# Masked cross-attention: the last key's term taken per group on the extracted output instead of per batch by a product with the identity

## The chip, the cores and the metric

The kernel runs on one core of a Trainium2 chip. The metric is the device time of one execution in microseconds; the time given is the median of three runs. Nothing else runs on the core.

## The reference

A stack of six layers works on `x`, 128 batches of 32 tokens with 256 features (4096 tokens); only the first layer is changed here. It is an attention of the tokens on a context of 257 rows per batch, with 16 heads of 16 features:

```python
q = split_heads(layernorm(x) @ Wq + bq)        # 16 heads x 32 queries x 16
k = split_heads(ctx @ Wk + bk)                 # 16 heads x 257 keys x 16
v = split_heads(ctx @ Wv + bv)
scores = einsum('bhqd,bhkd->bhqk', q, k) / sqrt(16)
scores = where(mask > 0, -1e9, scores)
p = softmax(scores, axis=-1)
x = x + (einsum('bhqk,bhkd->bhqd', p, v) merged to 256) @ Wo + bo
```

After it come a state space layer, a quantized feed-forward layer, a second (sigmoid) attention on the same context, a self-attention and a layer of experts. Everything is float32 within a small tolerance.

## The kernel before

Each layer is one block of code in which every engine has its own instruction stream, written out by hand, and waits on semaphores that the others raise. Nothing is scheduled by a planner: the order on an engine is the order in the code. The changed layer is `masked_attention` (tiles print as `x_...`).

Of the 257 keys, 256 fill two tiles of 128, and the last (`LAST`) stands apart. Its key vectors (`kx`) and value vectors (`vx`) are computed once for all 128 batches in `last_keys`, before the loop. Its score comes from tiny products in `last_scores`, and `place_last` copies it as a 257th column into `prob`, so that the softmax covers it.

The batches go in groups of four, since 4 x 32 tokens fill 128 rows. The loop `for b in SLOTS` has one turn per batch, on every engine. A turn (a slot) on TensorE is: `scores(b)`, `keys(b + 2)`, `turn(b - 1)` (the transposes of the probabilities), `values(b)`, `attend(b - 2)`. By the batch's number in its group one piece of group work is put in: slot 0 has `output` (after the scores) and `xnT`, slot 1 `queries`, slot 2 `denominators`, slot 3 `last_scores`. Slots 0 and 2 have the extraction of two batches' outputs on ScalarE and VectorE (`extract`).

How the last key's value term gets into the output: GpSimd (`value_last`) multiplies the batch's row of `vx`, spread to all 128 partitions by a transfer (`load_vx`), by the probabilities of the last key; partition 32h + t of `prob` holds head h of a strip and query t. `attend` (L492 on) first does eight products of V with the transposed probabilities, adding up in PSUM (`psO`), and then four products of that `pv` tile with the identity, which transpose and add it. Each product is 64 output rows by 128 columns, in float32. `extract` then picks each head's own columns out of `psO` into `oT`. The softmax denominators come at the end: `shares` takes reciprocals of the row sums (`sm`), `spread_sums` on GpSimd spreads them with `eye_q` into `sums`, `denominators` multiplies `sums` by `head_rows` so that each share reaches the rows of its head in `psA`, and `normalise` on VectorE multiplies `oT` by `psA`. `hi_ob` and `lo_ob` split the result into two float16 parts, and `output` multiplies by Wo.

VectorE's turn is `minima(b)` (four instructions L656, which take scores, masks and the running minimum), the extraction, group work (slot 0: `shares`, `residual`, `to_add`, which makes the next group's masks in L692 and L693; slot 2: `normalise`), `take_pT`, in slot 1 `lo_q` and `ln`, then `lo_k(b + 2)`, and in slot 3 `lo_ob`. `keys(b + 3)` in the next slot of TensorE waits for that `lo_k`.

PSUM has one bank `psM`, of which `psA` is columns 0 to 255 and `psX` (the last key's scores) columns 256 to 271.

Of the kernel before, what the change touches and what calls it, by code (L numbers as in the profile page):

```python
# [178 lines left out]
def masked_attention(nc, d, xres, con, norm):  # L179
# [5 lines left out]
    with ExitStack() as ctx:  # L185
# [17 lines left out]
        vx32 = sb("vx32", [P, D], F32)  # L203
        vxr = [sb(f"vxr{n}", [P, GB, D], F32) for n in range(2)]
# [13 lines left out]
        pv32 = [sb(f"pv32_{n}", [P, D], F32) for n in range(3)]  # L218
        sums = sb("sums", [P, 4, GB, T], F32)
# [3 lines left out]
        vx_dram = nc.dram_tensor("x0_vx", (NB, D), F32, kind="Internal").ap()  # L223
# [7 lines left out]
        vx_out, vxr_in = sem("vx_out"), [sem(f"vxr_in{n}") for n in range(2)]  # L231
# [10 lines left out]
        pv_last, pv_mm, o_part, o_ext = sem("pv_last"), sem("pv_mm"), sem("o_part"), sem("o_ext")  # L242
# [6 lines left out]
        def batch(f, b):  # L249

            if 0 <= b < NB:
                f(b)
# [8 lines left out]

        def strips(t):
            return t.rearrange("p (r c) -> p c r", r=RG)
# [8 lines left out]
        def _(sync):  # L272
# [17 lines left out]
            def load_vx(g):  # L290
                wait(sync, pv_last, (g - 1) * GB)
                src = vx_dram[g * GB:(g + 1) * GB, :].rearrange("(a j) n -> a j n", a=1).to_broadcast([P, GB, D])
                sync.dma_start(vxr[g % 2][:], src).then_inc(vxr_in[g % 2], 16)

# [3 lines left out]
            sync.wait_ge(vx_done, 1)  # L298
            sync.dma_start(vx_dram, vx32[:]).then_inc(vx_out, 16)
            sync.wait_ge(vx_out, 16)  # L300
            load_vx(0)
            for g in range(1, NT):
                if g + 1 < NT:
                    load(g + 1)
                load_mask(g)
                load_vx(g)

        @block.gpsimd
        def _(pool):
# [22 lines left out]
            def place_last(b):  # L332
                pool.wait_ge(last_done, b // GB + 1)
                wait(pool, t_mm, b - NP + 1)
                wait(pool, pv_last, b - NP + 1)
                pool.tensor_copy(prob[b % NP][:, :, LAST], lastv[b // GB % 2][:, b % GB, :]).then_inc(placed, 1)

            def value_last(b):
                g, j = b // GB, b % GB
                pool.wait_ge(exp_done, b + 1)  # L340
                pool.wait_ge(vxr_in[g % 2], 16 * (g // 2 + 1))
                wait(pool, pv_mm, b - 2)
                pool.tensor_tensor(pv32[b % 3][:].rearrange("p (c r n) -> p c r n", c=C, r=RG),
                                   vxr[g % 2][:, j, :].rearrange("p (c r n) -> p c r n", c=C, r=RG),
                                   strips(prob[b % NP][:, :, LAST]).unsqueeze(3).to_broadcast([P, C, RG, 64]), ALU.mult)\
                    .then_inc(pv_last, 1)

            def spread_sums(g):
# [4 lines left out]
                                   ALU.mult).then_inc(sums_done, 1)  # L353

# [14 lines left out]
            for b in SLOTS:  # L369
                g, j = b // GB, b % GB  # L370
                batch(value_last, b - 1)
# [10 lines left out]
        def _(pe):  # L382
# [9 lines left out]
            def last_keys():  # L392
                pe.wait_ge(last_lo, 1)
                for h in range(C):
# [4 lines left out]
                products(psV[:, 0:D], [part(lastp, lambda x: x[:, cc, :]) for cc in range(C)],  # L399
                         [part(W["v"], lambda w: w[:, cc, :]) for cc in range(C)]).then_inc(vx_mm, 1)  # L400
# [17 lines left out]
            def denominators(g):  # L418
                pe.wait_ge(sums_done, g + 1)
                wait(pe, q_lo, min(g + 3, NT))  # L420
                for r in range(RG):
                    last = pe.matmul(psA[64 * r:64 * r + 64, :], head_rows[:],
                                     sums[:, 2 * r:2 * r + 2].rearrange("p c j t -> p (c j t)"), start=True, stop=True)
                last.then_inc(sum_mm, 1)
# [66 lines left out]
            def attend(b):  # L491
# [3 lines left out]
                pe.wait_ge(pv_last, b + 1)  # L495
                if b % 2 == 0:
                    wait(pe, o_ext, b // 2)
                for kt in range(2):
                    for c in range(C):
                        to = (c * 2 + b % 2) * P  # L500
                        for r in range(RG):
                            s = r * C + c
                            pe.matmul(psO[64 * r:64 * r + 64, to:to + P],  # L503
                                      V[b % NV][:, kt, c * P + 64 * r:c * P + 64 * r + 64], pT[b % NW][:, kt, s * P:(s + 1) * P],
# [2487 lines left out]
```

## Time and profile before

| | |
|---|---|
| median of 3 runs | 3067.11 us (3064.57 to 3067.53) |
| the profiled execution | 3058.71 us, span 3056.9 us |
| TensorE busy in the span | 2633.2 us (86%) |
| VectorE, ScalarE, GpSimd busy | 2019.7, 1814.4, 1652.4 us |
| the changed layer | about 30 to 909 us of the span |
| its loop at a steady pace | about 80 to 880 us |
| mean granted TensorE clock | 0.926 of full speed |

The span runs from the first to the last instruction of the profiled execution. The line numbers L... are those of the kernel before. A row of the timeline gives an instruction's start and duration in microseconds, or those of several that follow one another (x2, x8). A float32 product of TensorE stands as two records. The duration of a matmul record includes the way through the array, so the time that one takes from the next is the distance of their starts.

### The profile page before, as it was taken

How to read it: one execution, taken by the hardware profiler on the slowest of the kernel's cores; microseconds unless marked ns; L12 is line 12 of the kernel's file. 1: busy time of each engine (PE TensorE's matmuls, PEld its weight loads, DVE VectorE, ACT ScalarE, POOL GpSimd, SP SyncE). 2: the span in 40 equal slices, each digit the busy share in tenths (PEclk: the TensorE clock that was granted, in tenths of full speed). 3: DMA queues.
4: the chain of work that ended last, by engine and by line, in shares of the span. 5: the costliest groups of instructions: out<-in, count | busy, mean ns of one | idle time of the engine just before them, and what ended most of it. 6: DMA issues, size and time to landing. Idle time of an engine off the chain costs nothing. (4 is left out here: it accounts for less than half of the span.)

```text
span 3056.9 us, 81164 instructions
## 1 busy us (share of the span) xinstructions
PE 2633.2 (86%) x31182; PEld 2052.3 (67%) x31182; DVE 2019.7 (66%) x4510; ACT 1814.4 (59%) x4252; POOL 1652.4 (54%) x1589
## 2 busy tenths in 40 slices
PE   2999999999985988986797999999994888527998
PEld 2888888888863655553355888888873666416776
DVE  4677777777764777776346777777766888653443
ACT  2667767667666777772345777777763666343333
POOL 3666666666635777773006666666644777142332
PEclk9999999999996999887798999999996999558999
DMA  5333332223300000000002212221200000451110
GB/s 145 85 84 85 84 82 76 75 77 84 92 28 1 1 1 1 1 1 14 16 15 84 64 49 64 64 64 49 64 18 16 2 2 2 170 181 48 38 40 26
DMA packets 120951, 160.04 MB, mean 52 GB/s; under 512 B 11456, under 2 KB 107840, under 8 KB 118400
## 3 DMA queue, kind: packets, MB, share of 16 engines
q1 hardware_dynamic: 115904, 140.28, 16.1%
q0 software_dynamic: 4672, 14.57, 1.3%
q8 instruction: 258, 4.23, 0.6%
q14 instruction: 117, 0.96, 0.1%
HBM read 139.99 MB, written 14.83 MB: 51 GB/s over the span
## 5 line engine op out<-in xcount | busy, mean ns | idle before, releaser
L570 ACT ACTIVATE x_prob<-x_prob,x_nm 128x257 f32<-128x257 f32 x512 | 254.5, 499 | 212.7 <-DVE x_nm L656 212.7
L1894 DVE TENSOR_TENSOR_SCAN m_s<-m_a,m_psD 128x1024 f32<-128x1024 f32 x128 | 284.9, 2267 | 3.0 <-PE m_psD L1721 2.9
L656 DVE CUSTOM_DVE_ANT_0 x_prob<-x_psS,x_masked,x_lastv 128x256 f32<-128x256 f32 x512 | 217.3, 481 | 104.0 <-PE x_psS L476 100.7
L1195 DVE SCALAR_TENSOR_TENSOR x_pTl<-x_psS,x_pTh 128x1024 f16<-128x1024 f32 x128 | 156.7, 1225 | 144.9 <-ACT x_pTh L1103 144.9
L1833 ACT ACTIVATE m_a<-m_dt,m_rate 128x248 f32<-128x248 f32 x512 | 206.9, 493 | 0.0
L2778 ACT ACTIVATE e1t_g<-e1t_psH,e1t_bias 128x128 f32<-128x128 f32 x312 | 89.2, 368 | 171.1 <-PE e1t_psH L2727 171.1
L1605 POOL TENSOR_TENSOR m_s<-m_s 128x1024 f32<-128x1024 f32 x64 | 150.6, 2354 | 68.5 <-DVE m_s L1894 68.5
L883 POOL TENSOR_TENSOR x_qbdh<-x_qh,all_mask4h 128x1024 f16<-128x1024 f16 x32 | 60.6, 1894 | 215.8 <-DVE x_ql L1176 215.8
L1116 ACT ACTIVATE x_vh<-x_psV 128x512 f16<-128x512 f32 x128 | 76.4, 597 | 134.4 <-PE x_psV L922 134.4
L875 POOL TENSOR_TENSOR x_ctxl<-x_ctx,x_ctxh 128x512 f16<-128x512 f32 x128 | 149.7, 1170 | 10.7
L318 POOL TENSOR_TENSOR x_ctxl<-x_ctx,x_ctxh 128x512 f16<-128x512 f32 x128 | 148.3, 1159 | 10.7
L386 PE MATMUL x_psK<-x_ctxh,x_wkh 128*128 128x256 f16 x512 | 142.1, 278 | 13.0 <-DVE x_kl L669 9.8
L2727 PE MATMUL e1t_psH<-e1t_xnh,e_wh 128*128 128x128 f16 x624 | 142.8, 229 | 3.2 <-issue 2.6
L922 PE MATMUL x_psK<-x_ctxh,x_wkh 128*128 128x256 f16 x512 | 141.4, 276 | 4.0 <-POOL x_ctxl L875 3.5
L1097 ACT ACTIVATE x_psS<-x_psS 128x1024 f32<-128x1024 f32 x128 | 129.0, 1008 | 24.1 <-PE x_psS L1016 24.1
L386 PE MATMUL x_psK<-x_ctxh,x_wkl 128*128 128x256 f16 x512 | 141.2, 276 | 0.0
L386 PE MATMUL x_psK<-x_ctxl,x_wkh 128*128 128x256 f16 x512 | 141.2, 276 | 0.0
L922 PE MATMUL x_psV<-x_wvh,x_ctxh 128*128 128x256 f16 x512 | 140.8, 275 | 0.0
L922 PE MATMUL x_psK<-x_ctxh,x_wkl 128*128 128x256 f16 x512 | 140.2, 274 | 0.0
L922 PE MATMUL x_psK<-x_ctxl,x_wkh 128*128 128x256 f16 x512 | 140.2, 274 | 0.0
L503 PE MATMUL x_psO<-x_pT,x_v 128*64 128x128 f32 x2048 | 140.0, 279 | 0.1
L386 PE MATMUL x_psV<-x_wvh,x_ctxh 128*128 128x256 f16 x512 | 139.6, 273 | 0.0
(591 smaller groups left out, 10617.9 us busy)
## 6 DMA issues: line engine op xcount, KB each, us to landing
x_ctx<-in_ctxT SPq DMA_DIRECT2D x64, 1024.0 KB, 6.2
x_mraw<-in_mask SPq DMA_DIRECT2D x128, 128.5 KB, 6.0
x_vxr<-x_vx SPq DMA_DIRECT2D x32, 512.0 KB, 6.9
e1r_stage<-in_L_ffn_w SPq DMA_DIRECT2D x16, 1024.0 KB, 5.0
e_rows<-e1r_pad POOLq DMA_DIRECT2D x1, 5070.0 KB, 19.6
e1t_row<-e_rows SPq DMA_DIRECT2D x39, 130.0 KB, 2.1
all_xres<-in_x SPq DMA_DIRECT2D x1, 4096.0 KB, 14.4
x_vxr<-x_vx SPq DMA_DIRECT2D x128, 32.0 KB, 3.5
```

The lines of the kernel that those rows point to most:

```text
L318: pool.tensor_tensor(lo[:, j], src, hi[:, j], ALU.subtract).then_inc(ctx_split, 1)
L386: last = pe.matmul(out, a, b, start=m == 0, stop=m == len(prods) - 1)
L503: pe.matmul(psO[64 * r:64 * r + 64, to:to + P], V[b % NV][:, kt, c * P + 64 * r:c * P + 64 * r + 64], pT[b % NW][:, kt, s * P:(s + 1) * P] ...
L570: last = act.activation(prob[b % NP][:, s, :], prob[b % NP][:, s, :], ACT.Exp, bias=nm[b % NP][:, s:s + 1], scale=-1.0, accum_out=sm[b // ...
L656: dve.tensor_tensor_reduce(prob[b % NP][:, s, 0:LAST], psS[:, s * LAST:(s + 1) * LAST], masked[g % 2][:, j, :], -SC, lastv[g % 2][:, j, s: ...
L875: pool.tensor_tensor(lo[:, j], src, hi[:, j], ALU.subtract).then_inc(ctx_split, 1)
L922: last = pe.matmul(out, a, b, start=m == 0, stop=m == len(prods) - 1)
L1195: dve.scalar_tensor_tensor(pT[c % 4][1][:].rearrange("p r k n -> p (r k n)"), psS[c % 2][:], PS, pT[c % 4][0][:].rearrange("p r k n -> p ( ...
L1605: pool.tensor_tensor(lower, lower, upper, ALU.add).then_inc(half_done, 1)
L1833: last = act.activation(A[k % 3][:, :, m, 1:T], dt[n % 2][:, h, :].rearrange("p (j t) -> p j t", t=T)[:, :, 1:T], ACT.Exp, scale=rate[:, h ...
L1894: dve.tensor_tensor_scan(states, rates, psD[at % 2][:], 0.0, ALU.mult, ALU.add).then_inc(scan_done, 1)
L2727: last = pe.matmul(bank[:, k % 4 * P:(k % 4 + 1) * P], a, b, start=m == 0, stop=m == len(prods) - 1)
```

## The change

The last key's value term is no longer added in `attend`. Instead:

- `take_last` on GpSimd copies the last key's four probabilities per row of each batch into `plast`, in the place of `value_last`.
- `spread_sums` has a second instruction: it spreads `plast` with `eye_q` into `lasts`, as `sm` into `sums`.
- `denominators` has two more products, `lasts` by `head_rows`, into columns 256 to 511 of `psM`, and one more wait.
- `normalise` first multiplies these columns by the value vectors `vx` of the group (now kept with features on the partitions) into `term`, adds `term` to `oT`, and then multiplies by the shares as before; each of the three waits for the one before it.
- `attend` has eight products instead of twelve and one wait less.
- `last_keys` makes `vx` with 12 products of 128 columns instead of 6 of 256, ScalarE copies it in two instructions, and the transfers to memory and back (`load_vx`) are gone.

```diff
-        vx32 = sb("vx32", [P, D], F32)
-        vxr = [sb(f"vxr{n}", [P, GB, D], F32) for n in range(2)]
+        vx = sb("vx", [P, NT, C, GB], F32)
...
-        pv32 = [sb(f"pv32_{n}", [P, D], F32) for n in range(3)]
-        sums = sb("sums", [P, 4, GB, T], F32)
+        plast = [sb(f"plast{n}", [P, GB, 4], F32) for n in range(2)]
+        sums, lasts = sb("sums", [P, 4, GB, T], F32), sb("lasts", [P, 4, GB, T], F32)
+        term = sb("term", [P, C, GB, T], F32)
...
-            def load_vx(g):
-                wait(sync, pv_last, (g - 1) * GB)
-                src = vx_dram[g * GB:(g + 1) * GB, :].rearrange("(a j) n -> a j n", a=1).to_broadcast([P, GB, D])
-                sync.dma_start(vxr[g % 2][:], src).then_inc(vxr_in[g % 2], 16)
...
-            def value_last(b):
-                g, j = b // GB, b % GB
+            def take_last(b):
                 pool.wait_ge(exp_done, b + 1)
-                pool.wait_ge(vxr_in[g % 2], 16 * (g // 2 + 1))
-                wait(pool, pv_mm, b - 2)
-                pool.tensor_tensor(pv32[b % 3][:].rearrange("p (c r n) -> p c r n", c=C, r=RG),
-                                   vxr[g % 2][:, j, :].rearrange("p (c r n) -> p c r n", c=C, r=RG),
-                                   strips(prob[b % NP][:, :, LAST]).unsqueeze(3).to_broadcast([P, C, RG, 64]), ALU.mult)\
-                    .then_inc(pv_last, 1)
+                pool.tensor_copy(plast[b // GB % 2][:, b % GB, :], prob[b % NP][:, :, LAST]).then_inc(taken, 1)
...
+                pool.wait_ge(taken, (g + 1) * GB)
+                pool.tensor_tensor(lasts[:], eye_q[:].unsqueeze(1).unsqueeze(1).to_broadcast([P, 4, GB, T]),
+                                   plast[g % 2][:].rearrange("p j s -> p s j").unsqueeze(3).to_broadcast([P, 4, GB, T]),
+                                   ALU.mult).then_inc(lasts_done, 1)
...
-                batch(value_last, b - 1)
+                batch(take_last, b - 1)
...
-                products(psV[:, 0:D], [part(lastp, lambda x: x[:, cc, :]) for cc in range(C)],
-                         [part(W["v"], lambda w: w[:, cc, :]) for cc in range(C)]).then_inc(vx_mm, 1)
+                for h in range(C):
+                    last = products(psV[:, h * NB:(h + 1) * NB],
+                                    [part(W["v"], lambda w: w[:, cc, h * P:(h + 1) * P]) for cc in range(C)],
+                                    [part(lastp, lambda x: x[:, cc, :]) for cc in range(C)])
+                last.then_inc(vx_mm, 1)
...
+                pe.wait_ge(lasts_done, g + 1)
                 wait(pe, q_lo, min(g + 3, NT))
-                for r in range(RG):
-                    last = pe.matmul(psA[64 * r:64 * r + 64, :], head_rows[:],
-                                     sums[:, 2 * r:2 * r + 2].rearrange("p c j t -> p (c j t)"), start=True, stop=True)
+                for to, src in ((0, sums), (256, lasts)):
+                    for r in range(RG):
+                        last = pe.matmul(psM[64 * r:64 * r + 64, to:to + 256], head_rows[:],
+                                         src[:, 2 * r:2 * r + 2].rearrange("p c j t -> p (c j t)"), start=True, stop=True)
                 last.then_inc(sum_mm, 1)
...
-                pe.wait_ge(pv_last, b + 1)
...
-                            pe.matmul(psO[64 * r:64 * r + 64, to:to + P],
-                                      V[b % NV][:, kt, c * P + 64 * r:c * P + 64 * r + 64], pT[b % NW][:, kt, s * P:(s + 1) * P],
-                                      start=b % 2 == 0 and kt == 0 and c == 0, stop=False, skip_group_check=True)
-                for c in range(C):
-                    to = (c * 2 + b % 2) * P
-                    for r in range(RG):
-                        last = pe.matmul(psO[64 * r:64 * r + 64, to:to + P],
-                                         pv32[b % 3][:, c * P + 64 * r:c * P + 64 * r + 64], con["ident"][:],
-                                         start=False, stop=True, skip_group_check=True)
+                            last = pe.matmul(psO[64 * r:64 * r + 64, to:to + P],
+                                             V[b % NV][:, kt, c * P + 64 * r:c * P + 64 * r + 64],
+                                             pT[b % NW][:, kt, s * P:(s + 1) * P],
+                                             start=b % 2 == 0 and kt == 0 and c == 0, stop=kt == 1, skip_group_check=True)
...
-            act.activation(vx32[:], psV[:, 0:D], ACT.Copy).then_inc(vx_done, 1)
+            for h in range(C):
+                last = act.activation(vx[:, :, h, :], psV[:, h * NB:(h + 1) * NB].rearrange("p (g j) -> p g j", j=GB), ACT.Copy)
+            last.then_inc(vx_done, 1)
...
             def normalise(g):
                 dve.wait_ge(sum_mm, g + 1)
                 dve.wait_ge(o_ext, 2 * g + 2)
+                dve.wait_ge(vx_done, 1)
+                dve.tensor_tensor(term[:].rearrange("p c j t -> p (c j) t"), psM[:, 256:512].rearrange("p (n t) -> p n t", t=T),
+                                  vx[:, g].rearrange("p c j -> p (c j)").unsqueeze(2).to_broadcast([P, C * GB, T]), ALU.mult)\
+                    .then_inc(term_done, 1)
+                dve.wait_ge(term_done, g + 1)
                 row = oT[g % 2][:].rearrange("p c j t -> p (c j t)")
+                dve.tensor_tensor(row, row, term[:].rearrange("p c j t -> p (c j t)"), ALU.add).then_inc(term_added, 1)
+                dve.wait_ge(term_added, g + 1)
                 dve.tensor_tensor(row, row, psA, ALU.mult).then_inc(o_norm, 1)
```

The order of instructions around two places, as the two kernels have it (line numbers in the second of each pair are those of the changed kernel). First GpSimd at the begin of a group (slot 0), before the change; `x_ctxh` and `x_ctxl` are the split of the context, `x_prob<-x_lastv` is `place_last`:

```order
L351 TENSOR_TENSOR x_sums<-x_eye_q,x_sm 128x512 [waits x0_sum_mm,x0_share_done]
L336 COPY x_prob<-x_lastv 128x4 [waits x0_pv_last,x0_t_mm,x0_last_done]
L343 TENSOR_TENSOR x_pv_2<-x_vxr,x_prob 128x256 [waits x0_pv_mm,x0_vxr_in0,x0_exp_done]
L316 TENSOR_SCALAR x_ctxh<-x_ctx_1 128x512 [waits x0_v_mm,x0_ctx_in1]
L318 TENSOR_TENSOR x_ctxl<-x_ctx_1,x_ctxh 128x512 [waits x0_ctx_hi]
L358 TENSOR_TENSOR all_xres<-all_xres,x_bo 128x256 [waits x0_xn_done]
```

and with the change:

```order
L331 TENSOR_TENSOR x_sums<-x_eye_q,x_sm 128x512 [waits x0_sum_mm,x0_share_done]
L335 TENSOR_TENSOR x_lasts<-x_eye_q,x_plast 128x512 [waits x0_taken]
L322 COPY x_prob<-x_lastv 128x4 [waits x0_taken,x0_t_mm,x0_last_done]
L326 COPY x_plast<-x_prob 128x4 [waits x0_exp_done]
L302 TENSOR_SCALAR x_ctxh<-x_ctx_1 128x512 [waits x0_v_mm,x0_ctx_in1]
L304 TENSOR_TENSOR x_ctxl<-x_ctx_1,x_ctxh 128x512 [waits x0_ctx_hi]
L342 TENSOR_TENSOR all_xres<-all_xres,x_bo 128x256 [waits x0_xn_done]
```

`x_lasts` is new behind `x_sums` and ahead of `place_last`, and the copy into `x_plast` stands where the product into `x_pv` stood. Then VectorE in slot 2, from the extraction to `lo_k`, before:

```order
L676 SCALAR_TENSOR_TENSOR x_oT<-x_psO,all_mask,x_oT 128x2x64 [waits x0_o_part] x3
L684 TENSOR_TENSOR x_oT<-x_oT,x_psM 128x256 [waits x0_o_ext,x0_sum_mm]
L663 COPY x_pT<-x_psT 128x512 [waits x0_pv_mm,x0_t_mm]
L669 SCALAR_TENSOR_TENSOR x_kl<-x_psK,x_bk,x_kh 128x256 [waits x0_s_mm,x0_k_hi]
L669 SCALAR_TENSOR_TENSOR x_kl<-x_psK,x_bk,x_kh 128x256
```

and with the change:

```order
L661 SCALAR_TENSOR_TENSOR x_oT<-x_psO,all_mask,x_oT 128x2x64 [waits x0_o_part] x3
L669 TENSOR_TENSOR x_term<-x_psM,x_vx 128x256 [waits x0_vx_done,x0_o_ext,x0_sum_mm]
L674 TENSOR_TENSOR x_oT<-x_oT,x_term 128x256 [waits x0_term_done]
L676 TENSOR_TENSOR x_oT<-x_oT,x_psM 128x256 [waits x0_term_added]
L648 COPY x_pT<-x_psT 128x512 [waits x0_pv_mm,x0_t_mm]
L654 SCALAR_TENSOR_TENSOR x_kl<-x_psK,x_bk,x_kh 128x256 [waits x0_s_mm,x0_k_hi]
L654 SCALAR_TENSOR_TENSOR x_kl<-x_psK,x_bk,x_kh 128x256
```

The two new instructions stand ahead of the multiplication by the shares; all that follows keeps its order.

## Rows read from the trace of the kernel before

**Rows 1.** Windows: length, each engine's busy us (instructions), clock, DMA share, GB/s.
```profile
80.00:880.00 800.00, 799.69 (x9763) 671.83 (x9760) 570.58 (x1857) 558.99 (x1736) 488.47 (x609) 1.00 0.30 80
880.00:906.00 26.00, 22.88 (x283) 18.85 (x280) 14.81 (x47) 14.27 (x45) 5.49 (x10) 1.00 0.01 2
```

**Rows 2.** Lines L351 and L336, GpSimd: count, ns min/median/max, first and last start.
```profile
L351 POOL TENSOR_TENSOR x_sums<-x_eye_q,x_sm x31: 1074/1077/1080, 92.8 to 879.8; 128x512 f32<-128x512 f32 x31
...
L336 POOL COPY x_prob<-x_lastv x125: 182/193/732, 81.7 to 886.6; 128x4 f32<-128x4 f32 x125
```

**Rows 3.** Grouped lines of the stage, TensorE: count | busy us, mean ns | idle before.
```profile
L509 PE MATMUL x_psO<-all_ident,x_pv 128*64 128x128 f32 x1008 | 76.5, 273 | 0.0
```

**Rows 4.** Timeline, TensorE, one group: start us, us, instruction.
```profile
402.92 0.61 PE L509 MATMUL x_psO<-all_ident,x_pv 128*64 128x128 f32 x8
403.46 0.28 PE L476 MATMUL x_psS<-x_kh,x_qbdh 64*128 64x256 f16 x2
...
410.91 0.28 PE L386 MATMUL x_psK<-x_ctxh,x_wkh 128*128 128x256 f16 x1
...
418.83 0.65 PE L422 MATMUL x_psM<-x_sums,x_head_rows 128*64 128x256 f32 x4
419.41 1.09 PE L487 MATMUL x_psT<-all_ident,x_prob 128*128 128x128 f32 x8
...
423.97 0.28 PE L386 MATMUL x_psK<-x_ctxh,x_wkh 128*128 128x256 f16 x1
...
429.70 0.28 PE L476 MATMUL x_psS<-x_kh,x_qbdh 64*128 64x256 f16 x2
...
430.46 0.28 PE L386 MATMUL x_psM<-x_woh,x_obh 128*128 128x256 f16 x1
```

**Rows 5.** Line L422, TensorE: count, ns min/median/max, first and last start.
```profile
L422 PE MATMUL x_psM<-x_sums,x_head_rows x128: 379/379/430, 103.9 to 903.8; 128*64 128x256 f32 x128
```

**Rows 6.** Timeline, GpSimd, the same group.
```profile
407.42 1.08 POOL L351 TENSOR_TENSOR x_sums<-x_eye_q,x_sm 128x512 f32<-128x512 f32 x1 [4.33 <-DVE x_sm L688]
408.44 0.73 POOL L336 COPY x_prob<-x_lastv 128x4 f32<-128x4 f32 x1
...
420.34 1.16 POOL L318 TENSOR_TENSOR x_ctxl<-x_ctx,x_ctxh 128x512 f16<-128x512 f32 x1
```

**Rows 7.** Timeline, VectorE, the same group.
```profile
407.53 0.99 DVE L692 TENSOR_SCALAR x_mlast<-x_mraw 128x4 f32<-128x4 int32 x1
408.43 0.68 DVE L693 TENSOR_SCALAR x_masked<-x_mraw 128x1024 f32<-128x1024 int32 x1
409.04 0.68 DVE L663 COPY x_pT<-x_psT 128x512 f32<-128x512 f32 x1
409.64 0.86 DVE L669 SCALAR_TENSOR_TENSOR x_kl<-x_psK,x_bk,x_kh 128x256 f16<-128x256 f32 x2
...
419.26 1.12 DVE L676 SCALAR_TENSOR_TENSOR x_oT<-x_psO,all_mask,x_oT 128x128 f32<-128x128 f32 x3
420.48 0.42 DVE L684 TENSOR_TENSOR x_oT<-x_oT,x_psM 128x256 f32<-128x256 f32 x1
420.82 0.68 DVE L663 COPY x_pT<-x_psT 128x512 f32<-128x512 f32 x1
...
429.62 0.43 DVE L698 TENSOR_TENSOR x_obl<-x_ob,x_obh 128x256 f16<-128x256 f32 x1 [0.35 <-ACT x_obh L590]
```

**Rows 8.** Timeline near the stage's end, VectorE and TensorE.
```profile
898.81 0.42 DVE L698 TENSOR_TENSOR x_obl<-x_ob,x_obh 128x256 f16<-128x256 f32 x1 [2.05 <-ACT x_obh L590]
...
899.29 0.28 PE L386 MATMUL x_psM<-x_woh,x_obh 128*128 128x256 f16 x1 [1.20 <-DVE x_obl L698]
```

**Rows 9.** Line L2329, VectorE, in a later stage.
```profile
L2329 DVE SCALAR_TENSOR_TENSOR a_obl<-a_o,a_obh x32: 424/426/1101, 2356.1 to 2620.1; 128x256 f16<-128x256 f32 x32
```

**Rows 10.** Timeline in that later stage, GpSimd and VectorE.
```profile
2363.04 1.90 POOL L2004 TENSOR_TENSOR a_qbdl<-a_ql,all_mask4h 128x1024 f16<-128x1024 f16 x1
...
2364.11 1.10 DVE L2329 SCALAR_TENSOR_TENSOR a_obl<-a_o,a_obh 128x256 f16<-128x256 f32 x1 [0.48 <-ACT a_obh L2214]
```

More of the change, by code:

```diff
@@ L222, in masked_attention @@
         (obp,) = parts("ob", [P, C, P], 1)
-        vx_dram = nc.dram_tensor("x0_vx", (NB, D), F32, kind="Internal").ap()
         psK, psV, psO, psM = ps("psK", [P, 512]), ps("psV", [P, 512]), ps("psO", [P, 512]), ps("psM", [P, 512])
@@ L230, in masked_attention @@
         ctx_in, mask_in = [sem(f"ctx_in{n}") for n in range(2)], sem("mask_in")
-        vx_out, vxr_in = sem("vx_out"), [sem(f"vxr_in{n}") for n in range(2)]
         last_hi, last_lo, kx_mm, kx_hi, kx_lo, vx_mm, vx_done = (sem(k) for k in (
@@ L241, in masked_attention @@
             "s_mm", "s_min", "exp_done", "t_mm", "pt_first", "pt_second"))
-        pv_last, pv_mm, o_part, o_ext = sem("pv_last"), sem("pv_mm"), sem("o_part"), sem("o_ext")
+        taken, pv_mm, o_part, o_ext = sem("taken"), sem("pv_mm"), sem("o_part"), sem("o_ext")
+        lasts_done, term_done, term_added = sem("lasts_done"), sem("term_done"), sem("term_added")
         sums_done, sum_mm, share_done, o_norm, ob_ready, ob_hi, ob_lo = (sem(k) for k in (
@@ L260, in flat @@
             return t[:].rearrange("p a b -> p (a b)")
-        def strips(t):
-            return t.rearrange("p (r c) -> p c r", r=RG)
         def own_cols(h):
@@ L297, in _ @@
             load(1)
[L298 to L301, printed above, removed]
             for g in range(1, NT):
@@ L305, in _ @@
                 load_mask(g)
-                load_vx(g)
         @block.gpsimd
@@ L334, in place_last @@
                 wait(pool, t_mm, b - NP + 1)
-                wait(pool, pv_last, b - NP + 1)
+                wait(pool, taken, b - NP + 1)
                 pool.tensor_copy(prob[b % NP][:, :, LAST], lastv[b // GB % 2][:, b % GB, :]).then_inc(placed, 1)
-            def value_last(b):
-                g, j = b // GB, b % GB
+            def take_last(b):
                 pool.wait_ge(exp_done, b + 1)
-                pool.wait_ge(vxr_in[g % 2], 16 * (g // 2 + 1))
-                wait(pool, pv_mm, b - 2)
-                pool.tensor_tensor(pv32[b % 3][:].rearrange("p (c r n) -> p c r n", c=C, r=RG),
-                                   vxr[g % 2][:, j, :].rearrange("p (c r n) -> p c r n", c=C, r=RG),
-                                   strips(prob[b % NP][:, :, LAST]).unsqueeze(3).to_broadcast([P, C, RG, 64]), ALU.mult)\
-                    .then_inc(pv_last, 1)
+                pool.tensor_copy(plast[b // GB % 2][:, b % GB, :], prob[b % NP][:, :, LAST]).then_inc(taken, 1)
             def spread_sums(g):
```

## The prediction

> **What bounds the kernel now.** I read the windows first, to find which engine fills the stage that is changed. From 80 to 880 us the first attention runs at full TensorE clock; TensorE is busy 799.69 of 800 us, VectorE 570.58 and GpSimd 488.47 [rows 1]. So here a microsecond of matmuls is a microsecond of time, and work of another engine costs only where it makes TensorE wait. In the last 26 us TensorE has pauses: the stage drains, and less is to be gained. Then came single lines, for the rhythm and for prices [rows 2, 3, 5], the timeline of one group of four batches on three engines, for how near the others come to TensorE [rows 4, 6, 7], and a later stage for what the trace shows of one new operation [rows 9, 10]. The 31 `sums` of the stretch stand from 92.8 to 879.8, so a group takes 26.23 us [rows 2]; the scores of a group's first batch start at 403.46 and those of the next group at 429.70 [rows 4]. I call a group's four turns of the loop slots 0 to 3.
>
> **What is removed on TensorE.** The products with the identity stand as 8 records per batch, in pairs: two run side by side, each on its half of the output rows. The first starts at 402.92, the last ends 0.61 later, and one lasts 0.273, so first and last pair start 0.337 apart: three steps of 0.11 us. Four pairs are 0.44 us. The 0.10 that is left until the next slot's scores at 403.46 is the changeover, which stays, since the products before have the same shape [rows 3, 4]. The bounds are 0.34 (first to last start) and 0.54 (changeover gone too). I take 0.44: 4 x 0.44 = 1.76 us per group.
>
> **What is added on TensorE.** `denominators` gets two more float32 products of 256 columns per group: four records, two pairs. The two pairs that are there start at 418.83 and last 0.65; a record of the last lasts 0.379, so it starts 0.27 after the first. The next work starts at 419.41, which leaves 0.31 for the second pair and a changeover of 0.10: 0.21 [rows 4, 5]. A pair more is 0.21 to 0.27, and twice the columns of a pair above would be 0.22. I take 0.22, so 0.44 per group. Net on TensorE: -1.76 + 0.44 = -1.32 us per group, -41 us in 31 groups, if nobody makes it wait.
>
> **What is added elsewhere.** Per batch GpSimd exchanges a multiplication of 256 elements for a copy of 4, and per group it gets one more spread like `sums`, 1.08 us; such a copy takes 0.19, and 0.73 where it is held up [rows 2, 6]. It has idle time enough (312 of the 800 us), so only its order matters. VectorE gets two instructions in `normalise`, each waiting for the one before. Its extraction does three dependent ones in 1.12, so a semaphore between two instructions is small; I count 0.04. One of 256 elements lasts 0.42 [rows 7]. In the opening of the stage, which ends before 80 us, ScalarE has one more activation and TensorE the same columns in other shape, where other waits rule: nothing, at worst half a microsecond. The transfers that go (the value rows' way through memory and 32 broadcasts of them) end no wait of TensorE: nothing.
>
> **Three places where TensorE could now wait.** VectorE's release reaches TensorE 0.06 after its end: 898.81 + 0.42 to 899.29 [rows 8].
> First, `output` in slot 0 waits for `lo_ob`, which hangs on slot 3's transposes. It ends at 429.62 + 0.43 = 430.05, and the products start at 430.46 [rows 4, 7]. Between the transposes and these products lies one `attend`, now 0.44 shorter: 430.11 against 430.02 is a wait of 0.09.
> Second, `keys` in slot 1 waits for `lo_k` of slot 0, the end of VectorE's longest row: 409.64 + 0.86 = 410.50 against a start at 410.91. This too would become a wait of 0.09, but the wait at `output` lies in the same stretch and gives just that: 0.
> Third, `keys` in slot 3 waits for `lo_k` of slot 2, behind the longer `normalise`. I keep the old clock as it runs from `lo_q` in slot 1, since from there GpSimd works on without a pause, and its L318 stays at 420.34 to 421.50 [rows 6]. `normalise` starts at 420.48, and one shorter `attend` earlier at 420.04. `term` takes 0.42 + 0.04, and the addition of `term` is issued at 420.50, while L318 runs.
> What that means the trace shows in a later stage. VectorE's L2329 reads two SBUF tiles, as the new addition does. Alone it takes 426 ns; issued at 2364.11, under a GpSimd instruction of 2363.04 to 2364.94, it takes 1.10 and ends at 2365.21, 0.27 after the other [rows 9, 10]. L684, which reads one SBUF tile and PSUM, has its 0.42 at 420.48 with L318 running beside it [rows 7].
> The Trainium skill (SBUF — State Buffer, section Who interferes with whom) has this as a rule: a VectorE instruction with two SBUF inputs contends with a GpSimd instruction that reads SBUF, one with a single SBUF input does not. By it the first and the third instruction of the new `normalise` stay free and the addition waits, and the rows agree.
> So the addition ends at 421.77, the multiplication is issued at 421.81, `take_pT` 0.34 later (as from 420.48 to 420.82) at 422.15, `lo_k` 0.60 later (as from 409.04 to 409.64) at 422.75; it ends at 423.61, and TensorE may go at 423.67. TensorE comes to these `keys` at 423.97 less two `attend` (0.88) plus `denominators` (0.44): 423.53. The wait is 0.14. Without the blocking VectorE's row would end 0.85 earlier and there would be none; with the pieces above each 0.05 longer it would be 0.35. So 0 to 0.35.
>
> **Sum.** Per group -1.32 + 0.09 + 0.14 = -1.09 us, times 31: -34 us. The drain gains two attends in its last chain (0.88) and pays two VectorE instructions there (0.92): 0. The profiled execution's 3058.71 us (span 3056.9, and 1.8 around it) becomes 3025. The median of the runs is 8.4 higher, at 3067.1; the difference carries over: 3033 us.
>
> **Rivals.** (a) As above, 3033 us, with 3028 to 3040 as its own range: chance 0.45.
> (b) The addition isn't held up, or gets in just before L318, which starts only 0.16 before it. Only the 0.09 stays: 31 x 1.23 = 38 us, 3029; by the upper bound of a batch's saving (0.54) it would be 12 us less, 3017. For it speaks how little shift is needed; against it that any delay of VectorE up to 1 us keeps it inside L318. Chance 0.22.
> (c) A further wait of 0.3 to 0.8 us per group somewhere: all margins above are used up, and what was hidden is now passed on. 31 x 0.55 = 17 us given back, 3050. Against it: the groups repeat so evenly that a delay has to have a cause, and I see none. Chance 0.18.
> (d) The other side, at the masks of slot 0. `sums` on GpSimd (407.42 to 408.50) holds up L692, issued at 407.53, until 408.52; then L693 gets in before GpSimd's copy issued at 408.44, which lasts 0.73 for that [rows 6, 7]. Now `lasts` (1.08) stands first in GpSimd's queue there, and the copy behind it. If `lasts` gets in before L693, VectorE's full row of slot 0 ends 1.08 later and so does the start of `keys` in slot 1: -1.09 + 1.08 = 0 per group, 3067 us. If the copy (0.19) slips in as well, and the two new pairs cost 0.27 each, it is +0.28: 9 us more than before, 3076. The change is slower from 1.09 us of such delay per group. Against it: in the trace L693 starts before L692 has ended and wins, and `lasts` has a semaphore to look at first. Chance 0.09, of it 0.05 slower.
> By the Trainium skill (SBUF — State Buffer, section SBUF: two separate sides) the one that starts first has the shared port for its whole instruction and the other blocks. Under that rule L693, started at 408.43, keeps its place and (d) does not occur; the copy's 0.73 agrees.
> (e) The change doesn't do what it says: the products go, but the pace of a batch was that of another engine. Against it stand the 799.69 of 800. 3067 us, chance 0.06.
>
> **How the numbers follow.** 0.2%, 6 us, is about what a measurement of this kernel tells from no change. Faster are (a), (b) and (c): 0.85. Same are (e) and 0.04 of (d): 0.10. Slower: 0.05. The range from 3021 to 3055 holds (a), nearly all of (b) and most of (c), some 0.8.
>
> **What would show it.** A group takes 25.15 us instead of 26.24, and TensorE stays busy for all but some 0.2 us of it. The new addition in `normalise` lasts about 1.27 us instead of 0.42; TensorE waits some 0.14 for `lo_k` before the keys of slot 3 and less than 0.1 for `lo_ob`. L692 and L693 look as before, and `lasts` is stretched to some 1.75. An addition of 0.42 everywhere would be (b), a mask instruction L693 of 1.75 would be (d). The working is wrong if the four pairs take less than 1.7 us per group out of TensorE's row, or if TensorE waits at a place not named here.

## The result, and the profile after

The changed kernel takes 3034.91 us, the median of 6 runs (3026.62 to 3042.49), against 3064.76 for the kernel before (6 runs, 3057.07 to 3067.53). The ratio is 0.9904, with a 95% interval of 0.9881 to 0.9926: faster by about 1%, some 29 us, with the whole interval below 1. 3033 us was forecast.

Its profiled execution took 3034.97 us (before: 3058.71). The first view is the windows of the attention stage, with the same columns as [rows 1]. 760 us of the steady part:

```profile
80.00:840.00 760.00, 753.50 (x8766) 618.50 (x8764) 611.24 (x1886) 550.68 (x1710) 468.22 (x634) 1.00 0.24 63
```

TensorE, which was busy for all but 0.31 of 800 us [rows 1], now has pauses of 6.5 us in 760. VectorE is busier by 1.6 us per group (611.24 in 760 us against 570.58 in 800), about twice what the two new instructions take when they run alone (2 x 0.42).

How long a group of four batches takes shows in TensorE's timeline: it is the distance from the scores of its first batch to those of the next group's first (before: 403.46 and 429.70 [rows 4]). The rows are from one group after the change:

```profile
392.15 0.28 PE L465 MATMUL x_psS<-x_kh,x_qbdh 64*128 64x256 f16 x2
...
392.99 0.28 PE L370 MATMUL x_psM<-x_woh,x_obh 128*128 128x256 f16 x1
...
398.49 0.28 PE L465 MATMUL x_psS<-x_kh,x_qbdh 64*128 64x256 f16 x2
...
399.34 0.27 PE L370 MATMUL x_psK<-x_ctxh,x_wkh 128*128 128x256 f16 x1
...
404.63 0.28 PE L465 MATMUL x_psS<-x_kh,x_qbdh 64*128 64x256 f16 x2
...
406.81 0.65 PE L411 MATMUL x_psM<-x_sums,x_head_rows 128*64 128x256 f32 x4
407.29 0.60 PE L411 MATMUL x_psM<-x_lasts,x_head_rows 128*64 128x256 f32 x4
407.82 1.09 PE L476 MATMUL x_psT<-all_ident,x_prob 128*128 128x128 f32 x8
...
411.18 0.28 PE L465 MATMUL x_psS<-x_kh,x_qbdh 64*128 64x256 f16 x2
...
412.18 0.27 PE L370 MATMUL x_psK<-x_ctxh,x_wkh 128*128 128x256 f16 x1 [0.16 <-POOL x_ctxl L304]
...
417.46 0.28 PE L465 MATMUL x_psS<-x_kh,x_qbdh 64*128 64x256 f16 x2
```

This group takes 417.46 - 392.15 = 25.31 us, which is also the mean of the steady groups (26.24 before, 25.15 forecast). Its slots, from scores to scores, are 6.34, 6.14, 6.55 and 6.28; before they were 6.70, 6.50, 6.55 and 6.50, as medians of the steady groups. The products with the identity took 0.44 out of each slot, and the new pairs put 0.44 into slot 2. So what was given back is 0.08 in slot 0, 0.08 in slot 1 and 0.22 in slot 3. 31 groups at -0.93 are -29 us, and the layer ends at 879.4 instead of 908.6. Group by group this is 26.3 us from the scores of the 13th batch to those of the 125th (141.03 to 875.84 before, 139.05 to 847.57 after); the first three groups, slower than the rest in both kernels, gave 2.0, and the stage's end 0.9.

The same group on VectorE, with the columns of [rows 7]:

```profile
392.51 0.42 DVE L690 TENSOR_TENSOR x_obl<-x_ob,x_obh 128x256 f16<-128x256 f32 x1 [0.35 <-ACT x_obh L573]
...
396.23 0.98 DVE L684 TENSOR_SCALAR x_mlast<-x_mraw 128x4 f32<-128x4 int32 x1
397.13 0.68 DVE L685 TENSOR_SCALAR x_masked<-x_mraw 128x1024 f32<-128x1024 int32 x1
397.73 0.68 DVE L648 COPY x_pT<-x_psT 128x512 f32<-128x512 f32 x1
398.33 0.86 DVE L654 SCALAR_TENSOR_TENSOR x_kl<-x_psK,x_bk,x_kh 128x256 f16<-128x256 f32 x2
...
408.44 0.43 DVE L669 TENSOR_TENSOR x_term<-x_psM,x_vx 128x256 f32<-128x256 f32 x1
408.90 1.29 DVE L674 TENSOR_TENSOR x_oT<-x_oT,x_term 128x256 f32<-128x256 f32 x1
410.22 0.42 DVE L676 TENSOR_TENSOR x_oT<-x_oT,x_psM 128x256 f32<-128x256 f32 x1
410.56 0.68 DVE L648 COPY x_pT<-x_psT 128x512 f32<-128x512 f32 x1
411.16 0.87 DVE L654 SCALAR_TENSOR_TENSOR x_kl<-x_psK,x_bk,x_kh 128x256 f16<-128x256 f32 x2
```

And on GpSimd, as in [rows 6]:

```profile
396.12 1.07 POOL L331 TENSOR_TENSOR x_sums<-x_eye_q,x_sm 128x512 f32<-128x512 f32 x1 [4.57 <-DVE x_sm L680]
397.15 1.59 POOL L335 TENSOR_TENSOR x_lasts<-x_eye_q,x_plast 128x512 f32<-128x512 f32 x1
398.69 0.19 POOL L322 COPY x_prob<-x_lastv 128x4 f32<-128x4 f32 x1
...
408.75 1.16 POOL L304 TENSOR_TENSOR x_ctxl<-x_ctx,x_ctxh 128x512 f16<-128x512 f32 x1
```

The addition of the term (L674), issued at 408.90 under GpSimd's L304, lasts 1.29 us and ends at 410.19, 0.28 after L304 (409.91). Its neighbours L669 and L676, with one operand in PSUM, have their 0.43 and 0.42, the first of them partly under the same L304. The masks L684 and L685 look as before, and `lasts` is stretched to 1.59. Over the whole layer, one line, with count and ns min/median/max:

```profile
L674 DVE TENSOR_TENSOR x_oT<-x_oT,x_term x32: 424/1282/1289, 105.2 to 875.8; 128x256 f32<-128x256 f32 x32
```

How the late operand reaches TensorE is read at its weight loads:

```profile
392.99 0.10 PEld L370 LDWEIGHTS x_psM<-x_woh,x_obh 128*128 128x128 f16 x1 [0.29 <-DVE x_obl L690]
...
399.31 0.10 PEld L370 LDWEIGHTS x_psK<-x_ctxh,x_wkh 128*128 128x128 f16 x1 [0.28 <-issue]
...
405.38 0.10 PEld L370 LDWEIGHTS x_psK<-x_ctxh,x_wkh 128*128 128x128 f16 x1 [0.21 <-issue]
...
412.14 0.10 PEld L370 LDWEIGHTS x_psK<-x_ctxh,x_wkh 128*128 128x128 f16 x1 [0.41 <-issue]
```

`lo_ob` ends at 392.93 and its load starts 0.06 later. `lo_k` ends at 399.19 and at 412.03; the loads behind it start 0.12 and 0.11 later. At 405.38 nothing is waited for: the idle 0.21 is the ordinary changeover there. So 0.28 and 0.41 contain 0.07 and 0.20 of waiting (0.08 and 0.22 by the medians of the slots), and the 0.29 at `output` contains 0.08. "issue" names no releaser; the end of `lo_k` in VectorE's rows does. The releaser L304 that the matmul row of 412.18 names is a coincidence: in the first experiment below the wait goes although nothing is done to L304.

The later stages, whose code is the same, were together 5 us longer in this execution. 3 us of it lie in the state-space stage. Its windows, before and after:

```profile
914.00:1443.00 529.00, 439.83 (x2848) 278.28 (x2848) 371.30 (x342) 345.79 (x770) 360.80 (x270) 0.86 0.01 2
```

```profile
885.00:1417.00 532.00, 442.50 (x2848) 279.07 (x2848) 371.12 (x342) 345.86 (x770) 360.72 (x270) 0.85 0.01 2
```

The same 2848 matmuls took 2.7 us more of TensorE at a granted clock of 0.85 instead of 0.86, while the other three engines were busy as long as before. In another execution (experiment `e11_loads`) that stage had 0.84 and 449.09 us of TensorE. So single times scatter by several us in stages that the change doesn't touch. That is why below the length of a group is the measure, and the time of the whole kernel only its frame.

### The profile page after: what moved, and what is told of

It reads as the page before. It is cut to its first block and busy times, and to the rows that moved or that the text cites. A ratio compares the mean times of both kernels' runs of the same rounds, so it can differ in the third digit from the quotient of the medians.

```text
span 3033.1 us, 79255 instructions
## 1 busy us (share of the span) xinstructions
PE 2604.3 (86%) x30292; PEld 2011.3 (66%) x30292; DVE 2070.8 (68%) x4574; ACT 1814.6 (60%) x4253; POOL 1635.1 (54%) x1621
## 5 line engine op out<-in xcount | busy, mean ns | idle before, releaser
L304 POOL TENSOR_TENSOR x_ctxl<-x_ctx,x_ctxh 128x512 f16<-128x512 f32 x128 | 148.1, 1157 | 10.7
```

What stands on the lines that cost most here:

```text
L304: pool.tensor_tensor(lo[:, j], src, hi[:, j], ALU.subtract).then_inc(ctx_split, 1)
```

## The experiments

All are edits of the changed kernel but two (e4, e10), which start from the kernel before. In the code, arguments and slices are shortened. Slots are medians of the steady groups (those between 80 and 840 us of the span), in us; "group" is their mean length, "longest" the longest of them. Where the last column has a time, there was one run only, and nothing is concluded from that time. The intervals of the ratios overlap for most rows; the differences between experiments are read from the slots.

| kernel | slots 0 to 3 | group | longest | ratio to before, or one run |
|---|---|---|---|---|
| before | 6.70 6.50 6.55 6.50 | 26.24 | 26.25 | 1 |
| changed | 6.34 6.14 6.55 6.28 | 25.31 | 25.37 | 0.9904 (0.9881 to 0.9926) |
| e1_psum | 6.33 6.14 6.55 6.06 | 25.17 | 26.13 | 0.9885 (0.9864 to 0.9906) |
| e2_swap | 6.33 6.07 6.55 6.21 | 25.16 | 25.22 | 0.9877 (0.9858 to 0.9895) |
| e3_lasts_first | 6.33 6.14 6.55 6.27 | 25.31 | 25.40 | 0.9890 (0.9871 to 0.9909) |
| e4_noprod | 6.33 6.14 6.12 6.06 | 25.15 | 25.94 | 0.9884 (0.9863 to 0.9906) |
| e5_double | 6.33 6.14 6.98 6.06 | 25.52 | 25.60 | 3037.44 us |
| e6_masks | 6.33 6.06 6.55 6.06 | 25.01 | 25.01 | 0.9863 (0.9835 to 0.9891) |
| e7_hiob | 6.26 6.21 6.55 6.06 | 25.17 | 26.11 | 3030.45 us |
| e8_all | 6.47 6.06 6.55 6.06 | 25.15 | 25.41 | 0.9867 (0.9833 to 0.9901) |
| e9_best | 6.26 6.06 6.55 6.06 | 24.93 | 24.94 | 0.9842 (0.9828 to 0.9855) |
| e10_noprod_masks | 6.33 6.06 6.12 6.06 | 24.59 | 24.92 | 3011.25 us |
| e11_loads | 6.34 6.14 6.55 6.27 | 25.34 | 26.33 | 3045.92 us |

**e1_psum.** The term is written back into its PSUM place, so the addition has one operand in SBUF instead of two.

```diff
-dve.tensor_tensor(term, psM[:, 256:512], vx, ALU.mult)
+dve.tensor_tensor(psM[:, 256:512], psM[:, 256:512], vx, ALU.mult)
-dve.tensor_tensor(row, row, term, ALU.add)
+dve.tensor_tensor(row, row, psM[:, 256:512], ALU.add)
```

> The changed kernel, but the term is written back into PSUM (columns 256 to 511 of psM, in place), so that the addition in normalise reads one SBUF tile and PSUM instead of two SBUF tiles. Theory A (the addition is held up by GpSimd's instruction because both its inputs lie in SBUF, and TensorE's wait before the keys of slot 3 hangs on that): the addition lasts 0.42 us instead of 1.22 to 1.29, the wait before the keys of slot 3 (0.22) goes, and a group takes 25.09 us instead of 25.30: some 6 us less than the changed kernel, 0.988 of before. Theory B (those keys wait for GpSimd's split, whose end at 412.18 the profile names as the releaser): the addition gets short, but the group stays at 25.30. Theory C (three dependent VectorE instructions are simply too long there): the group stays at 25.2 or more.

```profile
L674 DVE TENSOR_TENSOR x_oT<-x_oT,x_psM x32: 420/422/422, 105.0 to 871.3; 128x256 f32<-128x256 f32 x32
```

The addition takes 422 ns everywhere, and slot 3 falls from 6.28 to 6.06, by just the 0.22 that was given back there. So that wait is the blocked addition's. The mean gains less (25.17 instead of the typical 25.09), since two groups took 26.12 and 26.13: in these VectorE waited 1.3 and 1.5 us for the masks. The table of waits (us in total, times, longest; 80 to 840 us) has for VectorE's wait on the masks, in the kernel before, in the changed kernel and here,

```profile
DVE x_mlast L692 <- DMA x_mraw<-in_mask: 3.1, 7, 0.8
```

```profile
DVE x_mlast L684 <- DMA x_mraw<-in_mask: 0.4, 2, 0.3
```

```profile
DVE x_mlast L684 <- DMA x_mraw<-in_mask: 4.5, 4, 1.5
```

The kernel before had such waits too, up to 0.8 us, and no group was longer for them.

**e2_swap.** In `keys`, TensorE looks at the semaphore that is late before the one that has long been reached.

```diff
 def keys(b):
-    pe.wait_ge(ctx_split, b + 1)
+    wait(pe, k_lo, b)
     if b == 0: pe.wait_ge(kx_lo, 1)
-    wait(pe, k_lo, b)
+    pe.wait_ge(ctx_split, b + 1)
```

> The changed kernel, with the two waits ahead of the key products in the other order: first for lo_k, then for the split of the context. In the changed kernel TensorE's weight load starts 0.11 to 0.12 us after lo_k's end, while output, whose late semaphore is the first of two, starts 0.06 after its own. Theory A (a release costs more where the late semaphore is the last one looked at): the waits before the keys of slots 1 and 3 get 0.05 each shorter, a group takes 25.20 us instead of 25.30, 3 us less in all. Theory B (the 0.12 belongs to the releasing instruction or to the products): the group stays at 25.30.

```profile
408.18 0.10 PEld L370 LDWEIGHTS x_psK<-x_ctxh,x_wkh 128*128 128x128 f16 x1 [0.36 <-DVE x_kl L654]
```

`lo_k` ended at 408.13 in this execution: 0.05 from its end to the load, against 0.11 to 0.12 before the swap. Slots 1 and 3 are shorter by 0.07 each, and nothing else moved. The waits that are left, 0.01 in slot 1 and 0.15 in slot 3, are those that the prediction gave (0 and 0.14), which had taken its 0.06 from `output`, where the late semaphore is the first of two.

**e3_lasts_first.** GpSimd spreads the last probabilities before the sums, not behind them: the test of the rival (d) from its other end.

```diff
 def spread_sums(g):
-    pool.wait_ge(share_done, g + 1)
     wait(pool, sum_mm, g)
-    pool.tensor_tensor(sums, eye_q, sm, ALU.mult)
     pool.wait_ge(taken, (g + 1) * GB)
     pool.tensor_tensor(lasts, eye_q, plast, ALU.mult)
+    pool.wait_ge(share_done, g + 1)
+    pool.tensor_tensor(sums, eye_q, sm, ALU.mult)
```

> The changed kernel, with the spread of the last key's probabilities (lasts) ahead of the spread of the reciprocals (sums) on GpSimd, so that it runs while GpSimd waits for VectorE, and no longer beside the mask instructions. Theory A (lasts costs nothing where it stands; it loses the port to the masks and nobody waits for it): lasts lasts 1.08 us instead of 1.59, the group stays at 25.30 us. Theory B (part of the missing 0.15 us per group is its place in slot 0): the group gets 0.08 or more shorter.

`lasts` takes 1.07 us instead of 1.59, and the group stays at 25.31. Where `lasts` stands on GpSimd is not on the path of this kernel (e8 shows one where it is).

**e4_noprod.** From the kernel before: the products with the identity are left out and nothing is put in their place, so the last key's value term is missing from the output.

```diff
-for c in range(C):
-    for r in range(RG):
-        last = pe.matmul(psO[...], pv32[b % 3][...], con["ident"][:], start=False, stop=True)
```

> The kernel before, without the four products with the identity in attend (the last key's value term is left out of the result; GpSimd still makes the pv tile and TensorE still waits for it). Theory A (a batch's products are worth 0.436 us, four pairs at 0.109, and the waits at output and at the keys of slot 1 come up at 0.08 each as in the changed kernel, while the short normalise gives none in slot 3): a group takes 26.24 - 1.74 + 0.16 = 24.66 us, 49 us less in all, 0.984 of before. Theory B (the changeover goes with them, 0.54 per batch): 24.2 us. Theory C (the waits were made by the change's other parts, GpSimd's copies and lasts): 24.50 us.

Slots 0, 1 and 2 are as after the change, less the two new pairs in slot 2: 6.55 - 6.12 = 0.43, the price of the pairs from the other side. Slot 3 has no wait, as in e1. But the mean group is 25.15, not the slots' sum of 24.65. In the waits:

```profile
DVE x_mlast L686 <- DMA x_mraw<-in_mask: 25.8, 26, 1.8
...
PEld x_psK L386 <- POOL x_ctxl L318: 10.9, 7, 1.6
```

The masks' transfer, issued when a buffer comes free, lands too late for a group this short: VectorE waits in 26 groups, and those in which it waits 0.9 us or more take 25.3 to 25.9 instead of 24.65. The second line shows some waits of TensorE for GpSimd's split of the context beside it; e10, which moves the masks and nothing else, has neither. So this was not the clean price of the products that it was meant to be; e10 is.

**e5_double.** With e1's edit, the two new products of 256 columns are issued twice. The second time overwrites the first (`start=True`), so the result is the same and only TensorE's work grows.

```diff
-for to, src in ((0, sums), (256, lasts)):
+for to, src in ((0, sums), (256, lasts), (256, lasts)):
```

> The kernel with the term in PSUM, and the two products of lasts in denominators issued twice (same result). It prices an added pair where nothing is waited for: by the distance of starts 0.218 a pair, so slot 2 takes 6.99 instead of 6.55 us and a group 25.52 instead of 25.09. If an added pair costs 0.27 (as the first pair of such a row does) it is 25.63; if slot 2 has slack on TensorE that hides them, 25.1 to 25.3.

```profile
408.08 0.65 PE L411 MATMUL x_psM<-x_sums,x_head_rows 128*64 128x256 f32 x4
408.56 1.03 PE L411 MATMUL x_psM<-x_lasts,x_head_rows 128*64 128x256 f32 x8
409.52 1.09 PE L476 MATMUL x_psT<-all_ident,x_prob 128*128 128x128 f32 x8
```

From the first product of `lasts` to the next work there are 0.96 us with four pairs of records, 0.53 with two (407.29 to 407.82 above): 0.43 for two pairs, 0.215 each. Slot 2 grows by the same 0.43. 0.22 was taken.

**e6_masks.** With e1's edit, VectorE reads the masks of the next group in slot 1 instead of slot 0.

```diff
 # VectorE's order
-if j == 0: group(to_add, g + 1)
+if j == 1: group(to_add, g + 1)
```

> The kernel with the term in PSUM, and to_add (the next group's mask instructions) moved on VectorE from slot 0 to slot 1, ahead of take_pT, where VectorE waits over 1 us for TensorE. Theory A (the wait before the keys of slot 1 is VectorE's full row of slot 0, and the few long groups of the kernel with the term in PSUM, up to 26.12 us, are masks that land late for slot 0): that wait of 0.08 goes, the one at output (0.08) stays, slots take 6.34, 6.06, 6.55, 6.06, a group 25.01 us, and no group is longer; mean of the steady stretch 25.01 instead of 25.17. Theory B (the masks were late because the transfers themselves are the pace): long groups remain, mean above 25.1.

Slot 1 falls from 6.14 to 6.06, and every group is as long as the next (25.01, the longest 25.01). The masks have a slot more to land, and VectorE's row of slot 0, which sets `lo_k`, is 1.5 us shorter. The opening is shorter too. VectorE's first mask instruction of group 1, in the changed kernel and here:

```profile
67.45 0.17 DVE L684 TENSOR_SCALAR x_mlast<-x_mraw 128x4 f32<-128x4 int32 x1 [6.94 <-DMA x_mraw<-in_mask]
```

```profile
67.73 0.17 DVE L684 TENSOR_SCALAR x_mlast<-x_mraw 128x4 f32<-128x4 int32 x1 [1.96 <-DMA x_mraw<-in_mask]
```

The masks land at the same time, but VectorE has other work before it needs them. The scores of the 13th batch start at 130.82 instead of 139.05, 8 us earlier, of which shorter groups can explain less than one (three groups, 0.3 shorter each).

**e7_hiob.** With e1's edit, ScalarE computes `hi_ob` before the exponentials of slot 3.

```diff
 # ScalarE's order
+if j == 3: group(hi_ob, g - 1)
 batch(exps, b)
 ...
-if j == 3: group(hi_ob, g - 1)
```

> The kernel with the term in PSUM, and hi_ob in slot 3 moved on ScalarE ahead of the exponentials, where ScalarE waits over 2 us. Theory A (the wait at output shields the keys of slot 1): the wait at output (0.08) goes, but the keys of slot 1 now wait 0.16 instead of 0.08, since VectorE's row of slot 0 is what it was; slots 6.26, 6.22, 6.55, 6.06, a group stays at 25.09 us. Theory B (the two waits are independent): 25.01 us.

Slot 0 falls from 6.33 to 6.26: the wait before `output` is gone. Slot 1 rises from 6.14 to 6.21: the wait before its `keys` is now 0.15 instead of 0.08. So the first wait did shield the second, as the prediction had it, though not to nothing. The sum stays.

**e8_all.** All of e1, e2, e3, e6 and e7.

> The term in PSUM, masks in slot 1, hi_ob ahead of the exponentials, lasts ahead of sums, and the two waits ahead of the key products swapped. Theory A (the period is TensorE's own work once the three waits are gone): 26.24 - 1.74 + 0.44 = 24.94 us per group, all groups alike, TensorE idle nowhere; 31 x 1.30 = 40 us less than before in all, 0.987. Theory B (another engine or the transfers set a floor near 25.1): 25.1 or more, or groups of unequal length.

Slot 0 is 6.47, not 6.26. VectorE and GpSimd at the end of a slot 3:

```profile
332.10 0.88 DVE L654 SCALAR_TENSOR_TENSOR x_kl<-x_psK,x_bk,x_kh 128x256 f16<-128x256 f32 x2 [0.67 <-ACT x_kh L539]
332.89 0.99 DVE L690 TENSOR_TENSOR x_obl<-x_ob,x_obh 128x256 f16<-128x256 f32 x1
```

```profile
331.41 1.16 POOL L304 TENSOR_TENSOR x_ctxl<-x_ctx,x_ctxh 128x512 f16<-128x512 f32 x1
332.52 1.08 POOL L331 TENSOR_TENSOR x_lasts<-x_eye_q,x_plast 128x512 f32<-128x512 f32 x1
```

`lo_ob` (L690) reads two SBUF tiles. With `lasts` first it runs under GpSimd's L331 and lasts 0.99 instead of 0.42, until 0.28 after L331's end (333.60), and TensorE waits for it. The same blocking as at the addition, at another place, brought there by an edit that was harmless alone.

**e9_best.** e8 without e3's edit.

> The term in PSUM, masks in slot 1, hi_ob ahead of the exponentials, the two waits ahead of the key products swapped, and lasts behind sums again. In the version with lasts first, lo_ob (two SBUF inputs) took 0.99 us under lasts, and slot 0 took 6.47. Theory A (that is the whole of its miss): lo_ob lasts 0.42, slots 6.26, 6.06, 6.55, 6.06, a group 24.93 us, all alike; 0.987 of before. Theory B (another floor near 25.0): slot 0 stays at 6.33 or more.

```profile
80.00:840.00 760.00, 760.00 (x8906) 627.44 (x8902) 573.22 (x1917) 565.49 (x1737) 446.60 (x637) 1.00 0.24 62
```

TensorE has no pause left, and a group takes 24.93 us: 26.24 less four times 0.435 plus 0.43. The median is 3014.82 us of 5 runs, ratio 0.9842 (0.9828 to 0.9855): the fastest of the kernels that compute the whole reference. The layer ends at 858.8, 49.8 us earlier than before: 31 x 1.31 = 41 are the groups, some 7 the opening (three groups, beyond their 1.31 each) and 2 the last batches.

**e10_noprod_masks.** e4 with the masks in slot 1; the last key's value term is left out as there.

> The kernel before without the products with the identity (the last key's value term is left out of the result), and the mask instructions moved to slot 1. Without the move most groups waited for the masks' landing (25.8 us of idle time in front of them) and the mean group was 25.15 us against slots that add up to 24.65. Theory A (the masks' landing was the whole of the difference): slots 6.33, 6.06, 6.12, 6.06, a group 24.57 us, all alike. Theory B (with value_last kept, GpSimd is itself too late with the split of the context): TensorE waits for the split before the keys, mean above 24.8.

TensorE's scores at the starts of slots 1, 2, 3, 0 and 1:

```profile
383.08 0.28 PE L476 MATMUL x_psS<-x_kh,x_qbdh 64*128 64x256 f16 x2
...
389.14 0.28 PE L476 MATMUL x_psS<-x_kh,x_qbdh 64*128 64x256 f16 x2
...
395.26 0.28 PE L476 MATMUL x_psS<-x_kh,x_qbdh 64*128 64x256 f16 x2
...
401.32 0.28 PE L476 MATMUL x_psS<-x_kh,x_qbdh 64*128 64x256 f16 x2
...
407.65 0.28 PE L476 MATMUL x_psS<-x_kh,x_qbdh 64*128 64x256 f16 x2
```

24.57 us. Three slots are 0.44, 0.43 and 0.44 shorter than before, slot 0 is 0.37 shorter and waits 0.07 for `lo_ob`: the products cost 0.44 per batch. And 24.57 + 0.44 is e6's 25.01. VectorE no longer waits for the masks in any steady group, and TensorE no longer for the split of the context.

**e11_loads.** The transfers that the change took out are put back beside the changed kernel: the value rows through memory, and 32 broadcasts of them into a tile that nobody reads.

```diff
+sync.dma_start(vx_dram, vx)
 for g in range(1, NT):
     ...
+    sync.dma_start(vxr[g % 2], vx_dram[rows of g].to_broadcast([P, GB, D]))
```

> The changed kernel with the removed transfers put back (the value rows to memory, and 32 broadcasts of 512 KB into a tile that nobody reads). Theory A (they end no wait, as forecast): a group stays at 25.31 us and VectorE waits under 1 us in all for masks. Theory B (their removal kept the masks' landing ahead of the shorter groups): VectorE waits for masks in many groups, and the mean group is 25.5 or more.

The slots are the changed kernel's. The mean is 25.34 against 25.31: one group is 1 us longer. VectorE's waits for the masks rise from 0.4 to

```profile
DVE x_mlast L700 <- DMA x_mraw<-in_mask: 7.7, 13, 1.6
```

So the transfers cost about 1 us in this execution. The single time of 3045.92 says nothing against it: the state-space stage took 537 us of it at clock 0.84, against 532 at 0.85 in the changed kernel.

## Why the prediction was right, and where it was off

**The removed products: right.** 0.44 per batch, by e10's slots and by all others.

**The added products: right.** 0.22 per pair was taken; e5 gives 0.215, and e4 beside e1 gives 0.43 for both.

**The blocked addition: right, mechanism and size.** 1.27 was taken, 1.28 is the median. It is shown by e1, which gives it a PSUM operand and leaves all else as it was, and by e8, where the same thing happens to `lo_ob`. By the Trainium skill (SBUF — State Buffer, section Who interferes with whom) it is VectorE's two SBUF operands that meet GpSimd's reading; these rows agree with it at three lines: L674 1.28 against 0.42, L690 0.99 against 0.42, and L2329 1.10 against 0.43 [rows 9, 10]. The prediction's sentence on the rule leaves out a condition: the section exempts an instruction with one SBUF operand only outside VectorE's two-port modes. The mask instruction L684 has one such operand, and takes 0.98 beside `sums` (396.23) and 0.17 where it waited for its data (67.45). Rival (b) is out: only four of 32 additions took less than 1.27, two of them 0.42.

**The mis-sized term: the latency of VectorE's release.** The number came out, but one step of the working failed: "VectorE's release reaches TensorE 0.06 after its end" is not so for `keys`. The 0.06 came from `output` [rows 8] and holds there. `keys` looked at `k_lo` last of its semaphores, and there it is 0.12. That made the wait of slot 1 0.08 instead of 0 and that of slot 3 0.22 instead of 0.14, together 0.16 of a group's 25.31 us; the wait at `output` was 0.08, 0.09 was forecast. The group gained 0.93 instead of 1.09, and 31 x 0.16 = 5 us is what the layer's 29 falls short of the 34. e2 shows the step: with the order turned, the waits are 0.01 and 0.15, so 0.14 of the 0.16 hang on the order.

**The shielding of `keys` in slot 1 by the wait at `output`: right in kind, not to nothing.** e7 takes the wait at `output` away, and the next grows by as much (0.07).

**The drain of the stage: right.** From the last scores to the layer's end it was 15.1 (893.47 to 908.6), and is 15.2 (864.20 to 879.4).

**Rival (d): right that it would not occur.** L685 has its 0.68, L684 its 0.98, and e3 finds nothing to gain there. A detail was off: `lasts` is stretched to 1.59, where 1.75 was forecast; nobody waits for it.

**The transfers: nearly right.** About 1 us instead of nothing, by one execution (e11). What the prediction did not see is that the masks' landing had so little room: VectorE already waited for them 7 times in the kernel before, 3.1 us in all, hidden since its row had time to spare. For the changed kernel the room just suffices, and groups only 0.2 to 0.7 us shorter run into it (e1, e4, e7). So a wait like that of rival (c) stands one step beyond this change.

**The final number** lies nearer to the forecast, 3034.91 against 3033, than the saving does (29.9 between the two medians, 34 forecast). That is luck: all six runs of the kernel before have a median 2.3 us lower than the three that the prediction started from. The execution that was profiled took 3034.97 where 3025 was forecast: 5 us of that are the group's, and 5 the later stages'. What stays open is what sets the granted clock of the state-space stage, 0.84 to 0.86 with the same code.

## What to carry to other kernels

Where one engine is busy without a pause, price the edit by start-to-start distances in its timeline and then follow each semaphore that it waits for: the saving shows in full only as far as the others are ahead, here by some 0.35 us at two places. Give an addition on VectorE one operand in PSUM where GpSimd may be at work beside it, and let the waiting engine look first at the semaphore that will be late. After any gain look for the transfer that now has the least room, since the next edit will meet it: moving the masks by one slot brought the layer's end 12 us forward (874.9 to 863.1, e1 to e6), where the whole change brought 29.

## What the runs showed of the hardware that was not expected

- The release of a waiting TensorE took 0.05 to 0.06 us from the end of VectorE's instruction to the weight load when the late semaphore was waited for ahead of another (`output`, and `keys` in e2), and 0.11 to 0.13 when it was the last one (`keys` in the other kernels that wait there). Why is not shown. The order of two waits, which changes nothing else, was worth 0.14 us per group (e2).
- An addition or subtraction of 128x256 blocked by GpSimd ended 0.27 to 0.28 us after GpSimd's instruction, not with it: 410.19 against 409.91, 333.88 against 333.60 in e8, and 2365.21 against 2364.94 [rows 10].
- The blocking goes the other way too: `lasts` takes 1.07 us alone (e3) and 1.59 beside the mask instructions of VectorE.
- With the same code, TensorE's busy time for the 2848 matmuls of the state-space stage differed by 9 us between executions: 439.83, 442.50 and 449.09 us at granted clocks of 0.86, 0.85 and 0.84.
